# Odd states' sums of rows 0 to 2 added into the loaded rows at the end of the last row, in a decoder layer on one core

## What is computed

```python
def step(state, xs):                       # for each batch row, along the 512 positions
    d_t, B_t, C_t, u_t = xs
    dA = jnp.exp(d_t[..., None] * A)
    state = state * dA + (d_t * u_t)[..., None] * B_t[:, None, :]
    y_t = jnp.einsum('ben,bn->be', state, C_t)      # sum over the 16 states n
    return (state, y_t)
...
y = y + D[None, :, None] * u
y = y * jax.nn.silu(z)                     # z: the normalized attention result
...
x = _layernorm(x + _L0_attn_ref(...))
x = _layernorm(x + _L0_xattn_ref(ctx_1024, x, ...))
x = _layernorm(x + _L0_ffn_ref(...))
```

## Time and profile before

| | value |
|---|---|
| median of 3 runs | 1000.1 us |
| the profiled execution's own time | 997.59 us |
| span inside it | 995.8 us |
| TensorE (matmul) busy | 864.1 us, 87% |
| VectorE busy | 757.6 us, 76% |
| ScalarE busy | 674.1 us, 68% |
| GpSimd busy | 495.0 us, 50% |
| software queue (GpSimd's transfers) | 58.72 MB, 30.5% of the 16 DMA engines' span |
| hardware queue (SyncE's transfers) | 76.44 MB, 22.6% |
| `add_group` transfers, L1425 | 52 of 1 MB, 8.8 us from issue to landing (median) |
| `add_odd_sum` transfers, L1432 | 4 of 1 MB, 12.8 us (median) |

### The profile page before, as it was taken

The page is one execution under the profiler, slowest core; times in us unless marked ns, Lnnn a source line. Parts: engine busy times, 40 slices in busy tenths (PEclk is TensorE's granted clock), DMA queues, the critical chain, the costliest instruction groups (busy, mean ns, idle before and its releaser), DMA issues.

```text
span 995.8 us, 11868 instructions
## 1 busy us (share of the span) xinstructions
PE 864.1 (87%) x3824; PEld 624.7 (63%) x3824; DVE 757.6 (76%) x1053; ACT 674.1 (68%) x994; POOL 495.0 (50%) x458
## 2 busy tenths in 40 slices
PE   6879887797779778788878988899999999899997
PEld 3447544476445565446544566787777778688885
DVE  3797898875898859987678776888888888345542
ACT  4698985788956898659598365767777776242321
POOL 0079867897857979569999731122211221001000
PEclk9889788897679796997878989999999999999999
DMA  8167989589976799977999022111111110223211
GB/s 263 34 178 171 203 182 210 134 222 239 211 197 139 201 223 234 226 146 166 220 255 324 36 96 85 43 43 56 49 42 42 42 63 21 74 85 99 93 64 53
DMA packets 49907, 135.98 MB, mean 137 GB/s; under 512 B 5364, under 2 KB 13684, under 8 KB 41156
## 3 DMA queue, kind: packets, MB, share of 16 engines
q0 software_dynamic: 8064, 58.72, 30.5%
q1 hardware_dynamic: 40432, 76.44, 22.6%
q10 hardware_dynamic: 1364, 0.25, 0.2%
HBM read 57.93 MB, written 81.66 MB: 140 GB/s over the span
## 4 chain that ended last, share of the span: by engine, by line
PE 22%; issue 22%; DVE 14%; POOL 13%; DMA 9%; ACT 3%; DVEq 1%; ACTq 0%; POOLq 0%
DMA y_scratch<-state 9%; POOL state L1414 7%; PE banks L703 5%; PE banks L727 4%; PE banks L592 4%; DVE leaf L1194 3%; DVE w_gu L1194 3%; PE banks L630 3%; PE banks L639 3%; ACT leaf L984 2%; DVE state L1166 2%; PE banks L534 2%; POOL prod_a L1403 2%; POOL y_scratch L1425 1%; DVE idx_sb L1178 1%
## 5 line engine op out<-in xcount | busy, mean ns | idle before, releaser
L1414 POOL TENSOR_TENSOR state<-state,crep 128x512 f32<-128x512 f32 x256 | 350.7, 1658 | 67.5 <-DVE state L1166 67.5
L1166 DVE TENSOR_TENSOR_SCAN state<-decay,banks 128x512 f32<-128x512 f32 x256 | 296.5, 1204 | 73.8 <-PE banks L630 47.0
L703 PE MATMUL banks<-x2T,wgu 128*128 128x512 f32 x1056 | 246.5, 393 | 5.4 <-DVE hT L1244 4.0
L630 PE MATMUL banks<-ident,scaled 128*128 128x128 f32 x1024 | 175.5, 316 | 79.4 <-DVE state L1166 69.2
L630 PEld LDWEIGHTS banks<-ident,scaled 128*128 128x128 f32 x1024 | 138.2, 162 | 153.5 <-DVE state L1166 67.6
L703 PEld LDWEIGHTS banks<-x2T,wgu 128*128 128x128 f32 x1056 | 197.9, 189 | 52.9 <-DVE hT L1244 11.4
L876 ACT ACTIVATE decay<-delta,negA 128x512 f32<-128x512 f32 x256 | 171.0, 718 | 85.0 <-DVE state L1166 84.6
L865 ACT ACTIVATE scaled<-duT,BT 128x512 f32<-128x512 f32 x256 | 163.4, 716 | 0.0
L984 ACT ACTIVATE leaf<-idx_sb,table,table_gap 128x1024 f32<-128x1024 uint8 (+1 forms) x132 | 129.4, 1022 | 6.8 <-DVE w_down L1194 3.2
L1194 DVE COPY_PREDICATED leaf<-idx_sb,leaf 128x1024 f32<-128x1024 uint8 (+1 forms) x88 | 94.5, 1073 | 6.3 <-issue 5.5
L1497 POOL TENSOR_TENSOR pool_wait_here<-minus_half 128x1 f32<-128x1 f32 x22 | 4.3, 194 | 180.0 <-DVE w_gu L1194 115.4
(11 more groups left out here) (137 smaller groups left out, 1125.0 us busy)
## 6 DMA issues: line engine op xcount, KB each, us to landing
y_scratch<-state POOLq DMA_DIRECT2D x52, 1024.0 KB, 8.8
crep<-c_scratch SPq DMA_DIRECT2D x64, 256.0 KB, 5.7
idx_sb<-in_idx SPq DMA_DIRECT2D x11, 512.0 KB, 3.5
xT_sb<-in_xT SPq DMA_DIRECT2D x16, 256.0 KB, 4.5
y_scratch<-u SPq DMA_DIRECT2D x4, 1024.0 KB, 6.0
y_scratch<-state SPq DMA_DIRECT2D x4, 1024.0 KB, 6.3
y_scratch<-y_scratch POOLq DMA_DIRECT2D x4, 1024.0 KB, 12.8
leaf<-x_scratch SPq DMA_DIRECT2D x16, 256.0 KB, 2.8
```

Source lines behind the costliest of these rows:

```text
L630: last = nc.tensor.transpose(banks[:, k % NB, lc * LQ:(lc + 1) * LQ], scaled[:, g % SR, lc, et * P:(et + 1) * P], ident[:])
L703: last = mm(banks[:, 2 * tb + w, :], wgu[par][:, w, ws, t * P:(t + 1) * P], x2T[:, tb, xs, t, :], start=t == 0 and n == 0, stop=t == HT - ...
L1166: V.tensor_tensor_scan(state[:, g % GR, et, :], decay[:, k % DR_RING, :], banks[:, k % NB, :], 0.0, ALU.mult, ALU.add).then_inc(scan_ready, 1)
L1414: G.tensor_tensor(state[:, g % GR, et, :], state[:, g % GR, et, :], crep[:, g % CR, :], ALU.mult)\
```

## The change

The DRAM-to-DRAM add at (4, 0) of rows 1, 2 and 3 goes away. Instead SyncE loads rows 0 to 2 with even sums only, as soon as the last even group has been added. At the units (13, 0), (13, 3) and (14, 2) of row 3 GpSimd issues, for rows 0, 1 and 2, an accumulating transfer of 1 MB from `y2_scratch` into the loaded row in SBUF. The gates wait for this transfer (`odd_in`) instead of for the load. Row 3 keeps its DRAM-to-DRAM add.

```diff
+        odd_in = [sem(f"odd_in{b}") for b in range(S - 1)]
...
                 def load_row(b):
-                    sp.wait_ge(y_out, 16 * b + 16)
+                    if b < S - 1:
+                        sp.wait_ge(*group_sum(DS * b + DS - 2))
+                    else:
+                        sp.wait_ge(y_out, 16)
...
                 def gate_y(b):
                     dve.wait_ge(gate_ready, {0: 2, 3: 6}[b])
-                    dve.wait_ge(y_in[b], 16)
+                    if b < S - 1:
+                        dve.wait_ge(odd_in[b], 16)
...
+                def add_odd_to_row(b):
+
+                    pool.wait_ge(y_in[b], 16)
+                    pool.wait_ge(*group_sum(DS * b + DS - 1))
+                    pool.dma_start(taken[b][:, 0:ROW], y2_rows[:, b], accum_op=ALU.add).then_inc(odd_in[b], 16)
...
+                ODD_AT = {(13, 0): 0, (13, 3): 1, (14, 2): 2}
...
-                            if b and at == (4, 0):
-                                add_odd_sum(b - 1)
...
                             if not more and at == (11, 3):
                                 add_odd_sum(b)
+                            if not more and at in ODD_AT:
+                                add_odd_to_row(ODD_AT[at])
...
                 def gate_row(b):
                     pool.wait_ge(gate_ready, {1: 4, 2: 8}[b])
-                    pool.wait_ge(y_in[b], 16)
+                    pool.wait_ge(odd_in[b], 16)
```

## The result

The changed kernel takes 993.24 us (median of 4 runs, 992.95 to 994.95) against 999.9 us: ratio 0.9942, 95% interval 0.9923 to 0.9962. That is 5.8 us faster by the ratio and 6.7 us by the medians; 12.5 us were forecast. In a second set of runs, on the chip of experiments 5 to 8, the ratio was 0.9925 (0.9905 to 0.9944), 7.5 us. Its profiled span is 991.4 us, 4.4 us less than before.

A forecast was written before the change was run, and what follows sets the result against it. The ring of four state buffers coming free was taken to set the order of work, with scans waiting behind DRAM adds. 5.3 + 4.8 + 2.9 - 0.5 = 12.5 us, so median 1000.1 - 12.5 = 987.6 us; 8-in-10 range 982.5 to 996.5.

The forecast's parts named there:

- The add out of rows 1 and 2: VectorE's scans of state 7 in rows 1 and 2 stop waiting behind the DRAM add: gains 5.3 and 4.8 us.
- GpSimd's idle time of 5.71 us: Sign to check in row 1: GpSimd shows no idle time before the add that was at 237.75 us.
- Rival C: Waits in rows 1 and 2 stay because the DMA engines are full; about 996.0 us; chance 0.05.
- Row 3: Taking the DRAM add out of row 3 lets its last state add issue sooner: gain 2.9 us, bounds 1.6 and 9.5.
- The scan of group 59: Sign to check in row 3: this scan's 6.95 us wait for the last state add should still be 5 to 7 us.
- Rival D: Row 3's last state add also lands sooner, removing half or more of the 6.95 us wait; 981 to 984 us; chance 0.07.
- The price of an add into SBUF: At the end of row 3, each queued 1 MB add takes 5.5 us, like the state adds.
- A: Tail takes most of the gain: adds into SBUF at 10.8 us each, third 11.1 us late; 998.2 us; chance 0.12.
- B: Slower than before at `gate_row(2)` and `stage2_rstd(0)`: adds don't overlap, 14.2 us each; 1013.5 us; chance 0.11.
- The third add then lands at 543.4 + 5.1 + 3 x 5.5 = 565.0 us: End of row 3, old clock: own DRAM add lands, 5.1 us of other DMA work, then three adds; 0.3 us late.
- Who waits: Gates of rows 0 to 2 want the adds at 553.22, 558.06, 563.90 us; `stage2_rstd(0)` behind has 0.77 us to spare.
- The forecast cost of the end: Late adds into the loaded rows at the end of row 3 cost 0.5 us; bounds nothing and 11.1 us.

The follow-up runs named there:

- experiment 5: The changed kernel unaltered, run again on another chip, against the kernel before: 991.96 us, ratio 0.9925.
- experiment 6: The changed kernel with row 3's 1 MB of sums requested ahead of its 768 KB of attention results: 992.16 us, ratio 0.992 to the kernel before.
- experiment 7: The changed kernel with row 3's DRAM add and the three adds into rows requested 3 to 6 us earlier: 994.35 us, ratio 0.9947 to the kernel before.
- experiment 8: The changed kernel with row 2's add behind row 3's load and row 2's GpSimd gate behind `stage2_rstd(0)`: 991.93 us, ratio 0.9911 to the kernel before.
- experiment 1: The changed kernel without the three adds into loaded rows, gates waiting for the loads alone: 986.24 us, ratio 0.9872 to the kernel before.
- experiment 3: The changed kernel with only rows 0 and 1 moved, row 2's DRAM add staying at (4, 0) of row 3: 990.04 us, ratio 0.9898 to the kernel before.
- experiment 4: The changed kernel with the adds of rows 1 and 2 issued only once row 3's load has landed: 995.43 us, ratio 0.9962 to the kernel before.
- experiment 9: The changed kernel with the three adds into rows cut into 2 KB pieces instead of 8 KB: 988.3 us, ratio 0.9876 to the kernel before.
- experiment 11: The changed kernel with rows 0 and 1 added in DRAM at (11, 2) of the next row, only row 2 into its loaded row: 987.57 us, ratio 0.9879.
- experiment 2: The kernel before, all DRAM adds in place, with the three adds into loaded rows issued as well: 1004.73 us, ratio 1.005 to the kernel before.
- experiment 10: The changed kernel with the three transfers into rows as plain copies instead of adds: 989.47 us, ratio 0.9888 to the kernel before.

## Why the prediction was wrong

- *The add out of rows 1 and 2: right.* Forecast 5.3 and 4.8 us with 0.5 and 0.4 us of wait left. Row 1's distance fell by 5.1 us and row 2's wait by 4.6 us, with 0.48 and 0.41 us left before state 7 and 0.92 us before state 8 of row 1. One sign failed: GpSimd's idle time of 5.71 us shrank to 1.59 us and didn't vanish. Rival C is refuted, since the waits went, although the load of x landed sooner too (14.9 us after its issue, before 18.0).
- *Row 3: right in size.* From its first to its last scan row 3 takes 102.2 us, before 105.2, a gain of 3.0 us against 2.9 forecast. The scan of group 59 still waits, 5.85 us (5 to 7 expected), but 1.1 us of the gain is this wait getting shorter, which the prediction held fixed. Rival D, half or more of the 6.95 us, is out. That all rows together gained 13.0 us, the very sum 5.3 + 4.8 + 2.9, is in part luck: counted from row 1's first scan to the last of row 3 it is 12.1 us in this execution and 14.3 us in that of experiment 5.
- *The price of an add into SBUF: right.* They landed 5.7 us apart against 5.5 forecast. With the whole end 11.4 us earlier, A's third add would have landed at 564 us, or at 561 us with 8 us an add. It landed at 550.3 us, so rivals A and B are refuted as mechanisms.
- *"The third add then lands at 543.4 + 5.1 + 3 x 5.5 = 565.0 us": this step failed.* It put the plain load of row 3 ahead of the adds, as 5.1 us of work that they wait for. It was the other way round: the adds kept their 5.7 us and the load waited for them. The sum of the work was nearly right: everything had landed by 553.6 us, which is 565.0 on the old clock. That it agrees to the tenth is luck, since row 3's own DRAM add landed at 533.2 us, 1.2 us later than that clock gives, and the rest took 20.4 us where 21.6 were forecast. Which of the transfers came last was taken for granted.
- *"Who waits": this failed with it.* The list named the gates of rows 0 to 2 and `stage2_rstd(0)`, and not `rest_summed` on TensorE, whose load went from 6.9 to 19.9 us. Before the change it had about 10 us to spare (landed at 543.85 + 6.9 = 550.8 us, wanted at 560.9), and 13 us more were put on it. The forecast cost of the end was 0.5 us; it was 3.88 us of wait, 2.6 us of slow clock and 0.3 us elsewhere. Experiments 1, 3, 4 and 9 show that the load's landing makes TensorE's gap: when the starvation is eased in any of four ways, the gap goes. The list also left out the last load of C, for which GpSimd waited 1.73 us; in experiments 3 and 11 the late GpSimd alone cost 1.7 us.
- The time of 993.24 us lies inside the stated range (982.5 to 996.5), between the forecast and rival A in size, but by a mechanism that none of the rivals had. The gain is 5.8 us by the ratio and 6.7 us by the medians, against 12.5 forecast.

The difference adds up: 13.0 us gained by the scans, 1.6 us by which row 0 happened to start later in this execution (in experiment 5 it started within 0.4 us of before, and the span was 989.2 us), 6.8 us lost behind the last scan, leave 4.6 us; the span fell by 4.4.

## What to carry to other kernels

When a transfer is moved into a stretch, ask of every other transfer in that stretch when its consumer wants it, not only of the moved one: adding up the work of the DMA engines tells when all is done, not who is last. In this kernel a queue of 8 KB pieces starved a load of 2 KB pieces, and cutting the adds to 2 KB took the wait away (experiment 9); giving only the urgent load large pieces moved the loss to the next load (experiment 6). Look first for a place where the queue itself has a gap: the same add cost 4.5 to 5 us at state 4 of a row and nothing measurable at state 11.

## What the runs showed of the hardware

- Adds of 1 MB kept landing 5.7 us apart with a 1.75 MB plain load waiting beside them; the load's last part went from 6.6 us (no add) to 9.9, 14.8 and 19.9 us with one, two and three adds.
- Over the stretch of the backlog the two queues got about as many packets (393 to 445 with 8 KB pieces, 564 to 484 with 2 KB pieces). Elsewhere the plain queue got more, 511 to 212 in experiment 3 (535 to 546 us) and 544 to 163 in row 1 of the kernel before (222 to 231 us), so turn-taking by packet isn't the whole story; what sets the share is open.
- The last load of C, 256 KB, took 20.0 us beside the adds, and 13.6 us without them (experiment 1).
- 3.88 us of idle TensorE were followed by a granted clock of 0.50 from 554 to 557 us, and eight matmuls took 6.22 us in place of 3.60. In experiment 2 they took 5.40 us behind the same 3.88 us.
- The first two copies of experiment 10 landed 3.7 us apart and the third 6.1 us later, where adds land 5.7 us apart.
